# The last result of a masked attention kernel in two halves, by two engines and two queues

## The reference

```
scaler = jnp.float32(D) ** 0.5
q = target_key @ W_target.T
k = jnp.einsum('bld,ed->ble', item_keys, W_item)
v = jnp.einsum('bld,ed->ble', item_values, W_value)
scores = jnp.einsum('bd,bld->bl', q, k) / scaler
scores = scores + -100000000.0 * (1.0 - mask.astype(scores.dtype))
w = jax.nn.softmax(scores, axis=1)
return jnp.einsum('bl,bld->bd', w, v)
```

## Time and profile before

| what | us |
|---|---|
| median of 3 runs | 134.1 |
| lowest and highest of them | 133.74, 134.16 |
| the profiled execution, its own time | 133.42 |
| its span | 131.5 |
| TensorE busy | 70.4 |
| VectorE busy | 19.7 |
| ScalarE busy | 7.8 |

### The profile page before, as it was taken

The page is one execution under the profiler, slowest core; times in us unless marked ns, Lnnn a source line. Parts: engine busy times, 40 slices in busy tenths (PEclk is TensorE's granted clock), DMA queues, the critical chain, the costliest instruction groups (busy, mean ns, idle before and its releaser), DMA issues.

```text
span 131.5 us, 1317 instructions
## 1 busy us (share of the span) xinstructions
PE 70.4 (54%) x536; PEld 21.5 (16%) x536; DVE 19.7 (15%) x55; ACT 7.8 (6%) x26; POOL 5.3 (4%) x18
## 2 busy tenths in 40 slices
PE   0000005995499203983279601985359976459671
PEld 0000002331122001330012100322111322111150
DVE  6000000103300500004200310003300040330240
ACT  3000001000200000011100000000300001020000
POOL 7400000000100000000000000000100000010000
PEclk9999999999869995599559995589658999976998
DMA  8699896999699979997999799979899899999921
GB/s 273 273 547 461 359 491 280 498 498 452 296 498 488 452 311 483 498 452 311 483 483 452 327 483 467 452 343 483 366 436 436 381 428 454 443 407 417 409 87 30
DMA packets 2562, 53.22 MB, mean 405 GB/s; under 512 B 768, under 2 KB 768, under 8 KB 1024
## 3 DMA queue, kind: packets, MB, share of 16 engines
q1 hardware_dynamic: 2016, 53.07, 94.2%
q10 hardware_dynamic: 544, 0.13, 0.5%
HBM read 53.07 MB, written 0.13 MB: 404 GB/s over the span
## 4 chain that ended last, share of the span: by engine, by line
DMA 75%; PE 21%; SPq 1%; issue 1%; DVE 0%; ACT 0%; DVEq 0%
DMA value<-values 75%; PE ps_context L466 8%; PE ps_context L475 4%; PE ps_context L483 4%; PE ps_context L469 2%; PE ps_late L506 2%; PE ps_small L494 0%; SPq L209 0%; SPq L188 0%; PE ps_small L513 0%; SPq L205 0%; ACT result L295 0%; DVE context_late L401 0%; DVE context_t L409 0%; DVEq L408 0%
## 5 line engine op out<-in xcount | busy, mean ns | idle before, releaser
L447 PE MATMUL ps_scores<-first_tile,sta_query 128*32 128x400 f32 x256 | 29.9, 621 | 17.8 <-DMA first_tile<-keys 17.3
L466 PE MATMUL ps_context<-value,sta_full 128*32 128x512 f32 x64 | 13.5, 996 | 7.9 <-DMA value<-values 7.9
L447 PEld LDWEIGHTS ps_scores<-first_tile,sta_query 128*32 128x32 f32 x256 | 9.2, 132 | 37.1 <-issue 19.5
L431 PE MATMUL ps_small<-first_tile 64*64 64x128 f32 x4 | 0.7, 443 | 20.3 <-DMA first_tile<-first 20.3
L352 DVE SCALAR_TENSOR_TENSOR second_biased<-ps_scores,in_pair,mask_bias 128x200 f32<-128x200 f32 x4 | 1.7, 426 | 43.9 <-PE ps_scores L447 43.9
L391 DVE TENSOR_TENSOR context_slots<-ps_context,in_octet 128x512 f32<-128x512 f32 x4 | 2.8, 692 | 34.6 <-PE ps_context L483 28.1
L475 PE MATMUL ps_context<-value,sta_half 128*32 128x512 f32 x64 | 7.7, 598 | 0.4 <-DMA value<-values 0.4
L246 POOL COPY half_twice<-expd 128x128 f32<-128x128 f32 x4 | 1.4, 345 | 109.9 <-ACT expd L270 109.9
L453 PE MATMUL ps_turn_full<-ident,expd 128*128 128x128 f32 x4 | 1.4, 350 | 8.2 <-ACT expd L270 8.2
L483 PE MATMUL ps_context<-value,sta_full 128*32 128x512 f32 x48 | 5.7, 592 | 0.0
L466 PEld LDWEIGHTS ps_context<-value,sta_full 128*32 128x32 f32 x64 | 2.4, 158 | 14.4 <-DMA value<-values 9.1
(11 more groups left out here) (48 smaller groups left out, 33.0 us busy)
## 6 DMA issues: line engine op xcount, KB each, us to landing
value<-values SPq DMA_DIRECT2D x3, 6400.0 KB, 22.9
first_tile<-keys SPq DMA_DIRECT2D x2, 6400.0 KB, 20.7
first_tile<-first SPq DMA_DIRECT2D x1, 7024.0 KB, 19.5
first_tile<-keys SPq DMA_DIRECT2D x1, 3200.0 KB, 13.6
first_tile<-keys SPq DMA_DIRECT2D x2, 1600.0 KB, 18.7
value<-values SPq DMA_DIRECT2D x1, 2304.0 KB, 12.5
value<-values SPq DMA_DIRECT2D x1, 2048.0 KB, 17.0
value<-values SPq DMA_DIRECT2D x1, 1280.0 KB, 19.5
```

The lines of the kernel that those rows point to most:

```text
L447: last = nc.tensor.matmul(ps_scores[g * GU:(g + 1) * GU, 0:QB], window(sta_query, g, k), key[:, c:c + QB], start=k == 0, stop=k == QUADS - 1)
L466: nc.tensor.matmul(ps_context[g * GU:(g + 1) * GU, :], window(sta_full, g, k), value[:, c:c + OB], start=k == 0, stop=False)
```

## The change

The last block's scaling is done in two halves of 64 users. ScalarE scales users on partitions 0 to 63 and stores them from its queue (16 KB). VectorE, behind its last multiplication, scales those on partitions 64 to 127, and SyncE's queue, which waits for that, stores them (another 16 KB) and waits for the landing. Blocks 0 to 2 are scaled and stored as before. Two semaphores are new.

```diff
+HALF_P = P // 2
...
+        s_upper_result = sem("s_upper_result")
+        s_upper_stored = sem("s_upper_stored")
...
+            sp.wait_ge(s_upper_result, 1)
+            sp.dma_start(out_blocks[HALF_P:P, NBLK - 1], result[HALF_P:P, NBLK - 1]).then_inc(s_upper_stored, 16)
+            sp.wait_ge(s_upper_stored, 16)
...
             act.wait_ge(s_value_piece[len(CUTS) - 1], 16)
             store(0, NBLK - 1)
-            finish(NBLK - 1)
-            store(NBLK - 1, NBLK)
+
+            act.wait_ge(s_project, NBLK)
+            act.wait_ge(s_inv_sum, NBLK)
+            nc.scalar.activation(result[0:HALF_P, NBLK - 1, :], ps_project[0:HALF_P, :], ACT.Copy,
+                                 scale=inv_sum[0:HALF_P, NBLK - 1:NBLK]).then_inc(s_result, 1)
+            act.wait_ge(s_result, NBLK)
+            act.dma_start(out_blocks[0:HALF_P, NBLK - 1], result[0:HALF_P, NBLK - 1]).then_inc(s_stored, 16)
             act.wait_ge(s_stored, 16 * 2)
...
             keep_own_late()
+            dve.wait_ge(s_project, NBLK)
+            dve.wait_ge(s_inv_sum, NBLK)
+            nc.vector.tensor_scalar(result[HALF_P:P, NBLK - 1, :], ps_project[HALF_P:P, :],
+                                    inv_sum[HALF_P:P, NBLK - 1:NBLK], None, ALU.mult).then_inc(s_upper_result, 1)
```

## The result

The changed kernel is slower: 134.0 us (median of 20 runs) against 133.46 us (20 runs of the kernel before), a ratio of 1.0038 with a 95% interval of 1.0028 to 1.0049, or 0.5 us. The prediction had put 0.85 on no difference. The changed kernel's profiled execution took 133.95 us, with a span of 132.1; before it was 133.42 and 131.5.

What follows compares the result with a forecast made beforehand. Loads were taken to bound the kernel, with only the end behind the last product changing. The later landing, 131.21 against 131.18 us, added 0.03 us to the 134.1 us median, giving 134.1 us, range 133.6 to 134.7.

Steps and rivals of the forecast that it cites:

- What bounds the kernel: Loads take most time; nothing ahead of 129.31 us moves; last product to end 2.2 us before, 2.0 to 2.4 after.
- ScalarE's half: Last block's scaling on ScalarE: halving the partitions saves nothing, with bounds of 0.007 and 0.16 us.
- VectorE's half: Last block's scaling on VectorE: starts 0.10 us behind ScalarE, takes 0.22 us (0.20 to 0.43), ends at 129.65.
- two readers at a time: Both engines read one PSUM tile in the last scaling: sharing is worth 0.02 us, within the 0.22.
- ScalarE's store: ScalarE's last store: issue 0.02 us shorter, delay unchanged at 0.82 us, bytes 0.15 us; lands at 131.03, 0.15 us earlier.
- Two queues issuing at the same moment: The two last stores' issues at about 129.68: no cost, with a far end of +0.46 us.
- SyncE's queue: SyncE's last store: first byte 1.0 us behind its issue (0.82 to 1.0), landing at 131.21.
- A: Rival, chance 0.10: at the last stores' issue, SyncE's descriptors wait for ScalarE's, costing 0.46 us; +0.49 us in all, 134.6.
- B: Rival, chance 0.05: last block's scaling, issue and bytes all halve, so the end comes 0.48 us earlier, 133.6.
- C: Rival, chance 0.24: SyncE's store delay is 0.82 us, halves go out together, both land at 131.18; 0.00 us, 134.1.
- D: Rival, chance 0.11: longer program, one more queue awaited at the end or two more semaphores; at most +0.3 us, 134.4.
- The Trainium skill's rule on issuing engines: At the last stores: two issuers save only issuing time, second store's bytes gain nothing; +0.18 us in place of +0.03.

Runs made afterwards that it cites:

- lower_alone: The changed kernel without SyncE's last store, so only ScalarE's 64 rows of the last block are stored; ratio 1.0016 to the kernel before.
- two_full: The kernel before, with SyncE storing block 2 (128 rows) at the moment of ScalarE's last store of 128 rows; ratio 1.0030.
- sync_later: The changed kernel with SyncE's store held back by a VectorE memset of some 0.5 us; ratio 1.0079 to the kernel before.
- sync_load: The kernel before, with SyncE loading 64 rows from HBM into an unused tile at the moment of ScalarE's last store; ratio 1.0069.
- sync_store: The kernel before, with its last store of 128 rows issued by SyncE in place of ScalarE; ratio 1.0016.
- uneven: The changed kernel with the cut moved: ScalarE scales and stores 96 users, VectorE scales and SyncE stores 32; ratio 0.9998 to the kernel before.
- by_columns: The changed kernel with ScalarE scaling all 128 users and the two stores split by features, 128 rows of 32 each; ratio 1.0013 to the kernel before.
- steps_d: Awaited single stores of 64, 64, 63, 65, 72 and 56 rows added on ScalarE's queue behind the last block's store; 63 rows over in 1.34 us.
- steps_a to steps_d: Four runs adding awaited single stores of various shapes behind the last block's store; start to start 1.73 to 1.80 us behind 64 rows.
- upper_alone: The changed kernel without ScalarE's last store, so only SyncE's 64 rows of the last block are stored; ratio 1.0039 to the kernel before.

## Why the prediction was wrong

**What bounds the kernel** was right. The stretch up to the last product didn't move, and all of the loss is behind it. From the end of that product (129.30) to the end of the span it is 2.8 us, where the prediction had 2.0 to 2.4. That its 134.1 us stands near the measured 134.0 is luck: the three runs that it started from were 134.16, 133.74 and 134.1, all above 133.46, the median of the 20. The difference that it forecast was +0.03 us, and the measured one is 0.5.

**ScalarE's half, VectorE's half, two readers at a time:** right as to the end, by luck in VectorE's case, where two errors cancel. VectorE starts at 129.32, with ScalarE and not 0.10 us behind it, and takes 0.29 us, not 0.22. Nearer than the copies was the other operation with a per-partition scalar, 426 ns for 200 elements. The same ns per element and the same fixed part as in that row, (426 - 200 x 1.04) + 64 x 1.04, give 285 ns; an estimate, with 1.04 ns taken from 692 ns at 512 elements and 292 at 128 (400 / 384), the two-input operations of L391 and L401.

**ScalarE's store is the step that failed.** I had an issue of 384 rows at 0.43 us and one of 128 at 0.35, drew a line through them to 64, and got 0.02 us less and an unchanged delay of 0.82 us. The store of 64 rows takes 0.53 us to issue and begins to move 1.1 us behind it (lower_alone: issued at 129.70, first byte after 130.8). Alone it lands in 1.8 us, not in 0.82 + 0.15 + 0.38 = 1.35. Of these 0.45 us some 0.3 are the longer delay. The rest is mostly the bytes, which were to take half as long and move from 130.8 to 131.1, as long as those of 128 rows. Of the 0.48 us by which the last landing is late against before, 0.3 are from here.

**Two queues issuing at the same moment** was costed at 0, with a far end of 0.46 us. It is 0.2 us for the second: 2.0 against 1.8 us in the change, 1.7 against 1.5 in two_full, and nothing once the issues are 0.7 us apart (sync_later). By the one store of 128 rows in sync_load it is not a cost of every issue that has another beside it. In each of the pairs of stores it was ScalarE's that landed late, and SyncE's was issued with it or up to 0.02 us ahead; whether the order decides or the queue is not shown.

**SyncE's queue** was taken at 1.0 us to its first byte by a load's row. In shorter stretches nothing of that load moves before 32.4, so the row itself gives 1.1. A store from it moves as one from ScalarE's does: sync_store landed in 1.5 us. The term was wrong, and did no harm, since the longer delay of 64 rows stood on both queues.

**The rivals.** A gave the right size, +0.49 us, and was right that the queues interfere; but interference is 0.2 us of it, less than the 0.37 from which A was to decide, and its sign, SyncE's landing over 1.9 us behind its issue, did not come: it was 1.8. The change is over the bound only with the 0.3 us of the 64 rows, which no rival had, so that A's size fits is luck. B (the tail goes with the rows) is refuted for scaling, issue and landing alike. C has the right account of SyncE's queue but not of the halves going out together: in the change they go one behind the other. D is small: tails of 2.73 us with an additional queue awaited (sync_store) and 2.78 with both semaphores and queues (uneven) leave 0.14 us, or some 0.2 with the rounding of the spans, the interference included.

**The Trainium skill's rule on issuing engines** ("DMA: Bandwidth & Descriptors", "Issuing engines are not separate DMA queues") had given the better of my two sums, +0.18 us against +0.03. Its direction agrees with two_full and by_columns, +0.28 and +0.23 us of tail; that the shared engines are the reason is not shown, and it holds nothing on the 0.3 us of the 64 rows.

The Trainium skill's "DMA: Bandwidth & Descriptors" says in "Why a DMA increments its semaphore by 16 and not by 1" that a transfer is spread over the largest number of engines up to 16 that divides its row count; so 64 rows would use 16 of them, as 48, 80 and 128 do. The traces agree with the count. The page of steps_d has for ScalarE's queue:

```profile
q10 hardware_dynamic: 608, 0.13, 0.5%
```

These are 512 packets of rows and 96 more, and 96 is the sum of the rule's engines for its stores of 128, 64, 64, 63, 65, 72 and 56 rows (16 + 16 + 16 + 9 + 13 + 12 + 14). So the spread is not the cause: 16, 32, 48, 80, 96 and 112 rows would use 16 engines too and land in 1.4 us, where 64 rows take 1.8.

What stays open is why 64 rows are slow. The runs exclude the number of bytes, the number of features, the starting row, the queue, the place in the sequence and the spread over the engines as its cause, and go no further.

## What to carry to other kernels

By the rows of steps_a to steps_d a transfer's fixed cost isn't a smooth function of its shape: two measured sizes are no ground for a third, so look for a row of the very shape, or measure it by itself with a chain of awaited transfers. The last store of 32 KB is 1.2 us of delay and 0.3 of bytes here, so halving it has next to nothing to gain and a second queue's wait to lose. Where a small last store must be split, cut it at another count than 64 (96 and 32 here), and test one store alone before blaming the pair.

## What was not expected of the hardware

A store of 64 rows took 0.47 to 0.56 us to issue and 1.7 to 1.8 us to land when alone (lower_alone, upper_alone and the steps). Stores of 16, 32, 48, 80, 96 and 112 rows took 0.32 to 0.35 and 1.4 us, and one of 128 rows of 64 features 0.35 to 0.39 and 1.5. The load of 64 rows (sync_load) had the long issue too, 0.53 us. A store of 60 or 63 rows right behind one of 64 had an issue of 0.60 or 0.55 us though it landed in the ordinary time.

Two stores issued within 0.02 us on two queues landed 0.1 to 0.2 us apart, SyncE's as if alone and ScalarE's later. The scaling took ScalarE 0.31 us with 64, 96 or 128 partitions in use, and VectorE 0.29 us with 32 or 64.
